# Reordering the loads and the rounding of weights in the fill of an eight-stage software pipeline

## The reference, cut to what matters

```python
    x = x + _L0_attn_a_ref(_layernorm(x, axis=-1), ...)   # q, k, v, gate; scan over t; Wo; W1, gelu, W2
    x = x + _L0_ffn_ref(_layernorm(x, axis=-1), L0_ffn_router_w, L0_ffn_expert_weights)
    x = x + _L0_attn_b_ref(_layernorm(x, axis=-1), ...)   # h = tanh(x_t B + h A^T); y = h C W_out^T + b
    x = x + _L0_ffn_ref(_layernorm(x, axis=-1), L0_ffn_router_w, L0_ffn_expert_weights)

    # inside _L0_attn_a_ref
    h = _ln(x, ln_w, ln_b)
    ...
    x = x + o.reshape(Bb, Tt, HEADS * DV) @ Wo
    h2 = _ln(x, ln_w, ln_b)
    return x + jax.nn.gelu(h2 @ W1 + b1, approximate=False) @ W2 + b2
```

## Time and profile before

| | |
|---|---|
| median of three runs | 1781.47 us |
| the profiled execution | 1783.68 us, of it 1781.9 us from first to last instruction (the span) |
| PE busy | 1658.3 us, 93% of the span |
| DVE, ACT, POOL busy | 73%, 57%, 48% |
| mean granted TensorE clock | 0.966 of full |
| the chain that ended last, by engine | PE 76%, ACT 7%, DVE 5%, issue 5%, POOL 4%, DMA 1%, SP's queue 1% |
| DMA | 11.8% of 16 engines for SP's queue; 32 GB/s mean |

### The profile page before, as it was taken

How to read it: one execution, slowest core, us unless ns; L and a number is a source line. 1 busy time by engine, 2 the same in 40 slices (tenths; PEclk the granted TensorE clock), 3 DMA queues, 4 the chain that set the end, 5 groups by cost and what they waited for, 6 DMA issues and landing times.

```text
span 1781.9 us, 47524 instructions
## 1 busy us (share of the span) xinstructions
PE 1658.3 (93%) x15176; PEld 1406.3 (79%) x15176; DVE 1303.9 (73%) x4558; ACT 1009.2 (57%) x3694; POOL 858.7 (48%) x1293
## 2 busy tenths in 40 slices
PE   5488899999999999999999999999999999998876
PEld 3377788888888888888888888888888888887755
DVE  4456677787777777877778777787777777776554
ACT  4355566666565665655656656556566666554431
POOL 1355355554554555545545655455455554443211
PEclk8689899999999999999999999999999999999878
DMA  4211111011111110011111110111111101110000
GB/s 121 66 31 31 31 32 27 26 25 35 35 35 35 33 26 25 22 35 35 35 35 35 25 27 23 31 35 35 35 35 28 25 23 30 31 31 7 6 7 12
DMA packets 108174, 56.26 MB, mean 32 GB/s; under 512 B 73904, under 2 KB 107344, under 8 KB 107984
## 3 DMA queue, kind: packets, MB, share of 16 engines
q1 hardware_dynamic: 106464, 53.75, 11.8%
q10 hardware_dynamic: 1648, 1.72, 0.3%
HBM read 30.28 MB, written 16.78 MB: 26 GB/s over the span
## 4 chain that ended last, share of the span: by engine, by line
PE 76%; ACT 7%; DVE 5%; issue 5%; POOL 4%; DMA 1%; SPq 1%; ACTq 0%; POOLq 0%; DVEq 0%
PE ps L1130 57%; PE ps L1136 5%; PE ps L1173 4%; PE ps L1147 3%; PE ps L1198 2%; PE ps L1163 2%; PE ps L1161 2%; POOL r L386 1%; ACT ym L545 1%; PE ps L1417 1%; DVE hs L772 1%; DVE st L782 1%; PE ps L1193 1%; ACT ps L551 1%; ACT part L557 1%
## 5 line engine op out<-in xcount | busy, mean ns | idle before, releaser
L1130 PE MATMUL ps<-we,yT 128*128 128x512 f32 x3072 | 823.1, 412 | 0.0
L1130 PEld LDWEIGHTS ps<-we,yT 128*128 128x128 f32 x3072 | 548.4, 192 | 101.7
L539 ACT ACTIVATE h_lead<-ps 48x8 fp32r<-48x8 f32 x1024 | 174.4, 170 | 601.3 <-PE ps L1147 595.2
L772 DVE SCALAR_TENSOR_TENSOR hs<-ps,cst,h_lead 48x8 fp32r<-48x8 f32 x1024 | 222.7, 217 | 188.5 <-ACT ps L540 184.2
L1147 PEld LDWEIGHTS ps<-hs,aT 128*128 128x128 f32 x1024 | 196.2, 192 | 104.4 <-DVE hs L772 78.1
L1147 PE MATMUL ps<-hs,aT 128*128 128x8 f32 x1024 | 208.4, 204 | 38.5 <-DVE hs L772 37.9
L803 DVE SCALAR_TENSOR_TENSOR stage<-ps,coef,stage 128x256 f32<-128x256 f32 x384 | 184.1, 479 | 36.8 <-PE ps L1130 24.0
L414 POOL TENSOR_TENSOR part<-part 128x256 f32<-128x256 f32 x64 | 46.7, 730 | 332.7 <-ACT part L558 332.7
L803 DVE SCALAR_TENSOR_TENSOR acc<-ps,coef,acc 128x256 f32<-128x256 f32 x384 | 183.8, 479 | 12.4 <-POOL acc L416 5.3
L436 POOL TENSOR_TENSOR orstd<-omean,mhalf 128x32 f32<-128x32 f32 x32 | 174.1, 5440 | 2.7
L540 ACT ACTIVATE ps<-ps 48x8 f32<-48x8 f32 x1024 | 164.3, 160 | 0.0
(11 more groups left out here) (179 smaller groups left out, 3340.1 us busy)
## 6 DMA issues: line engine op xcount, KB each, us to landing
xin<-in_x SPq DMA_DIRECT2D x64, 128.0 KB
vrow<-vtok SPq DMA_DIRECT2D x32, 256.0 KB, 2.2
vx<-vrow SPq DMA_DIRECT2D x128, 64.0 KB, 2.0
sx<-smid SPq DMA_DIRECT2D x128, 64.0 KB
xag<-in_x SPq DMA_DIRECT2D x64, 128.0 KB
out<-stage SPq DMA_DIRECT2D x64, 128.0 KB
stage<-in_experts SPq DMA_DIRECT2D x1, 2048.0 KB, 8.9
stage<-in_Wvg SPq DMA_DIRECT2D x1, 512.0 KB, 5.3
```

What stands on the lines that cost most here:

```text
L539: a.activation(h_lead[:], ps[0:NB, BANK["RB"], k * B:(k + 1) * B], ACT.Tanh)
L772: v.scalar_tensor_tensor(hs[0:NB, :, k], h_whole, keeps_rest, h_lead[:].bitcast(F32), ALU.mult, ALU.subtract).then_inc(sem("rnn_h"), 1)
L1130: ins = t.matmul(dst, left(lp, c), right(rp, c), start=(n == 1), stop=(n == 3 * chunks))
```

## The change

Three things, all in the fill (iterations 0 to 4):

1. `load_x(xag, 0)` is issued right behind the early weights, ahead of the wait for them, and no longer in iteration 2.
2. SP's order. In iteration 1 xin of round 1 goes ahead of the last three late loads (`bin_`) and of the nine of A; in iteration 2 xin of round 2 goes ahead of the wait for `weights_rest` and of the load of the experts.
3. `split_experts` is cut in halves on ACT as well as on DVE: the first half in iteration 3, the second in iteration 4, at the same places of the two programs.

```diff
@@ -235,7 +235,7 @@
-        LEAD = {w: n + 1 for n, w in enumerate(("gate", "early", "recurrence_out", "late", "router", "experts"))}
+        LEAD = {w: n + 1 for n, w in enumerate(("gate", "early", "recurrence_out", "late", "router", "experts0", "experts"))}
@@ -310,12 +310,11 @@
             load_x(xin, 0, "x_loaded")
             for dst, src in early_sync:
                 sp.dma_start(dst, src).then_inc(sem("early"), 16)
+            load_x(xag, 0, "x_again")
             sp.wait_ge(sem("pads_zero"), 1)
             sp.wait_ge(sem("early"), EARLY)
-            for dst, src in late_sync:
+            for dst, src in late_sync[:6]:
                 sp.dma_start(dst, src).then_inc(sem("late"), 16)
-            for dst, src in recurrence_weights:
-                sp.dma_start(dst, src).then_inc(sem("a_loaded"), 16)
             sp.wait_ge(sem("spread_zero"), 1)
@@ -345,13 +344,18 @@
                     spread_state()
+                if live(it, 0) and not (isinstance(it, int) and it == 0):
+                    sp.wait_ge(sem("y0"), past(c0 - 1))
+                    load_x(xin, it, "x_loaded")
+                if isinstance(it, int) and it == 1:
+                    for dst, src in late_sync[6:]:
+                        sp.dma_start(dst, src).then_inc(sem("late"), 16)
+                    for dst, src in recurrence_weights:
+                        sp.dma_start(dst, src).then_inc(sem("a_loaded"), 16)
                 if isinstance(it, int) and it == 2:
                     sp.wait_ge(sem("weights_rest"), REST["late"])
                     sp.dma_start(stage[:].rearrange("p (c e d) -> p c e d", c=KC, e=E), wts["experts"]).then_inc(sem("experts"), 16)
-                if live(it, 0) and not (isinstance(it, int) and it == 0):
-                    sp.wait_ge(sem("y0"), past(c0 - 1))
-                    load_x(xin, it, "x_loaded")
-                if live(it, 2):
+                if live(it, 2) and not (isinstance(it, int) and it == 2):
                     sp.wait_ge(sem("res"), past(c2 - 1))
                     load_x(xag, it - 2, "x_again")
@@ -529,9 +533,10 @@
-            def split_experts():
+            def split_experts(c):
+                cols = slice(c * E * D, (c + 1) * E * D)
                 act.wait_ge(sem("experts"), 16)
-                a.activation(we[:, 0, :], stage[:], ACT.Copy).then_inc(sem("weights_lead"), 1)
+                a.activation(we[:, 0, cols], stage[:, cols], ACT.Copy).then_inc(sem("weights_lead"), 1)
@@ -682,8 +687,8 @@
-                    if isinstance(it, int) and it == 3:
-                        split_experts()
+                    if isinstance(it, int) and it in (3, 4):
+                        split_experts(it - 3)
@@ -773,7 +778,7 @@
-                dve.wait_ge(sem("weights_lead"), LEAD["experts"])
+                dve.wait_ge(sem("weights_lead"), LEAD["experts" if c else "experts0"])
@@ -969,9 +974,8 @@
-                    if isinstance(it, int) and it == 3:
-                        split_experts(0)
-                        split_experts(1)
+                    if isinstance(it, int) and it in (3, 4):
+                        split_experts(it - 3)
```

## The result

| | before | after |
|---|---|---|
| median of the runs | 1781.47 us | 1770.36 us (five runs, 1765.72 to 1771.34) |
| the profiled execution | 1783.68 us, span 1781.9 | 1765.72 us, span 1763.9 |
| PE busy | 1658.3 us, 93% | 1652.0 us, 94% |
| mean granted clock | 0.966 | 0.971 |

The ratio is 0.9932, interval 0.9917 to 0.9946: 11.1 us by the medians, 12.1 us by the ratio, 9.6 to 14.8 us by the interval. One of five runs of the kernel before (2021.09 us) and one of twelve of `e2_queue_order` (2017.77 us, at a mean granted clock of 0.74) fell in a slower state and are left out of every ratio; without them the two medians are 1781.25 and 1778.46 us. The forecast was 1768.0 us, 13.5 less.

A forecast was written before the change was run, and what follows sets the result against it. PE, 93% busy, bounds the whole span, but the chain through the first 120 us bounds the part changed. 10.2 + 0.6 + 3.7 - 1.0 = 13.5 us off the median 1781.5 gives 1768.0 us, range 1763.5 to 1773.

The forecast's parts named there:

- Part 1: Iteration 2, DVE's wait for xag of round 0: the early load lets `oss` begin 10.2 us earlier.
- Part 2: Iteration 1, xin of round 1 earlier and `bin_` later: 0.6 us gained, between +0.4 and +2.0.
- Part 3: Iteration 3, half the experts' rounding and subtraction: 3.7 us gained, limited by xag of round 1; bounds 2.2 and 3.9.
- Part 4: Iteration 4, where the experts' second halves come back: 1.0 us lost, bounds 0 and 2.2.
- 1.45 us are left over: Iteration 4: DVE's added 2.24 us subtraction ahead of `xmid`, less the 0.79 us of idle time before `yT`'s rest.
- The sum: Whole kernel: 10.2 + 0.6 + 3.7 - 1.0 = 13.5 us gained in the fill and carried to the end.
- near 102: Sign to look for in the changed profile: PE's first logits near 102 us.
- The early xag holds back the early weights: Rival, shared four DMA engines: late things move by up to 3.0 us, time 1770.2 us; chance 0.12.
- The clock of PE stays up: Rival, PE's work after the shortened idle gap runs at 2.4 GHz: time 1766.5 to 1765 us; chance 0.14.
- Given back in the fill: Rival, iterations 3 and 4: xag of round 1 or second halves cost their upper bounds, 1770.7 us; chance 0.09.
- Another wait takes the place: Rival, the stall of iteration 2: PE's attention or the experts end it, not xag; about 1780 us; chance 0.03.
- slower by the late weights: Rival, iteration 1: `bin_` landing after 35.2 us holds `scale_out` and loses the gain; 1786 us at 40; chance 0.02.

The follow-up runs named there:

- e2_queue_order: Kernel before with only SP's new order: xin of round 1 ahead of `bin_` and A, xin of round 2 ahead of the experts; 1778.91 us, ratio 0.9991.
- e1: Kernel before with only xag of round 0 issued early, behind the early weights; 1771.68 us, ratio 0.9954.
- e5: The changed kernel run once more, unedited, for the size of chance; 1770.56 us, ratio 0.9934.
- e4: Changed kernel without the halves of the experts' rounding, so early xag and SP's new order only; 1771.93 us, ratio 0.9953.
- e7: Changed kernel with both expert halves in iteration 3: ACT's behind the lead of `oTs`, DVE's behind `y1` and `ge`; 1768.4 us, ratio 0.992.
- e3: Kernel before with only the experts rounded in halves, in iterations 3 and 4; 1777.85 us, ratio 0.9984.
- e6: Changed kernel with `scale_out` moved from iteration 1 to iteration 2, behind `qt`; 1770.42 us, ratio 0.9928.
- e9: e7 with `scale_out` in iteration 2 and xag of round 1 issued ahead of xin of round 3; 1766.71 us, ratio 0.99.
- e10: e9 with DVE's two expert subtractions elsewhere in iteration 3, ahead of `att` and behind `y1`, away from POOL's `omean`; 1760.88 us, ratio 0.9892.

## Why the prediction was right, and where it was wrong

**Part 1, right.** The stall went whole, `oss` stood at 42.35 and waited for `osq`, as named. `e1` has 9.2 to 9.95 us in the traces where 10.2 were forecast. Its share in the time, 8.2 us, has 10.2 within its interval.

**Part 2, right.** The prediction had two ends: `scale_out` at 21.4 us, which leaves the 2.0, and `bin_` landing at 23.2, which leaves 0.45. It took 0.6, near the second. `scale_out` began at 22.47 in the first trace of the changed kernel, and at 23.23, 23.34 and 23.51 in the three others with parts 1 and 2 that leave it in its place (`e5`, `e4`, `e7`), each time behind a wait for `bin_`: the late landing is what happened. `kt` stood at 25.81, 26.58, 26.68 and 26.85 in these four, and at 26.71 to 27.11 in the four traces without either part, 0.3 us apart on average. The 1.3 us between the first two traces are the most favourable pair. At the first `orstd` the part is worth 0.94 us by `e4` against `e1`, and 1.5 and 1.7 by the two traces of the changed kernel, all in the range of +0.4 to +2.0.

**Part 3, right.** 3.7 us were forecast. The plain differences at the second `orstd`, 4.08 in `e3` and 4.59 in the changed kernel against `e4`, take in what the traces already differed by at the first. From the first `orstd` to the second it took 33.89 to 34.40 us in six traces with the experts rounded in one iteration, 34.19 in `e4`, and 30.37, 30.49 and 30.55 in the changed kernel, `e5` and `e3`. So the part is worth 3.3 to 4.0 us, and 3.8 against `e4`. (`e6`, with halves too but `scale_out` in iteration 2, took 31.64; why is open.) The wait for xag of round 1 that was named as late next is there, 2.62 us; it was forecast as some 2. `e9` took it away.

**Part 4, mis-sized.** The step was "1.45 us are left over", less 0.4 of PE's own attention: 1.0. PE waited 2.90 us for `yT`, against 0.71 and 0.76 without the halves, so the wait grew by some 2.2. Two things had been left out. The subtraction took 3.39 us and not 2.28, since POOL's `res` ran beside it:

```profile
95.27 1.27 POOL L496 TENSOR_TENSOR res<-xag,b 128x512 f32<-128x512 f32 x1
```

It was 3.39 in both traces of the changed kernel, and 3.35 in `e6`. In `e3`, where it lay beside `res` for 0.94 us (109.97 to 110.91), it took 3.08, 0.80 longer. No kernel moved `res` away from it, so this cause rests on how the lengths go together. And PE had nothing left to cover with: at a granted clock of 1.00 from 87 to 95 us, it ended its attention at 98.16, 2.90 ahead of the logits:

```profile
97.53 0.63 PE L1202 MATMUL ps<-vx,att 128*32 128x64 f32 x32
```

The full clock seems also to have paid it back, though no kernel tests this: from the second `orstd` to the first logits the changed kernel took 27.01 us (27.14 in `e5`), the kernel before 26.43 and 28.04 in its two traces, and `e4` 27.47, whose PE ran at 0.50 from 94 to 98 us:

```profile
94.00:98.00 4.00, 4.00 (x42) 3.86 (x42) 1.43 (x2) 0.00 (x0) 1.33 (x3) 0.50 0.44 84
```

So the wait was twice what was forecast, and no loss up to the logits stands clear of what two traces of one kernel differ by. That the sum held all the same is luck. A price for part 4 in time is not to be had from these runs: against the first trace of the kernel before it is 0.6 us in the changed kernel and 3.84 in `e3`, and which of them depends on where PE's clock was low.

**The sum.** At the first logits 14.60 us were won where 13.5 were forecast, and "near 102" was 101.06. The medians give 11.1, with 9.6 to 14.8 by the interval; 13.5 lies in it. The 2.4 us between forecast and median are no more than one run differs from the next.

**The rivals.** *The early xag holds back the early weights*: refuted in its size, up to 3.0 us, and not in its kind. ACT's early rounding began at 9.94 to 10.45 us in the five traces without the early xag, and at 10.64 to 11.40 in the eight with it. All eight are later than all five, by 0.8 us on average; the 0.19 us of the first pair is the smallest difference. It did not wait for all of xag: in the changed kernel it began at 10.64, while DMA still moved at the share of 0.27 to 0.28 that it had held from 8.5 us on (before, nothing moved from 10.0 to 10.5 us):

```profile
9.00:9.50 0.50, 0.00 (x0) 0.00 (x0) 0.16 (x2) 0.00 (x0) 0.14 (x1) 1.00 0.28 90
10.50:11.00 0.50, 0.00 (x0) 0.00 (x0) 0.00 (x0) 0.36 (x1) 0.32 (x2) 1.00 0.27 94
```

Of the prediction's two readings, a small delay and a wait of Wk for all of xag, the traces bear out the first, at 0.8 us. The sum had this cost at nothing; whatever it cost is contained in the 9.2 to 9.95 us of part 1. *The clock of PE stays up*: refuted where it was said. After a gap of 5.88 us (15.0 before) PE worked from 51.0 to 54.7 us at 0.50:

```profile
51.00:54.70 3.70, 3.47 (x11) 2.80 (x11) 0.93 (x3) 1.71 (x4) 3.22 (x9) 0.50 0.00 0
```

It stayed up elsewhere, around 90 us, for which no rival had been made, and in sum less time was spent at the lower level (the last section has the figures). *Given back in the fill*: part 4 alone was at its upper bound, and part 3 was not. *Another wait takes the place*, and *slower by the late weights*: no; `scale_out` was 1.1 to 2.1 us later than its 21.4 in the four traces, and 13.8 were needed.

## What to carry to other kernels

Moving a load forward wins the wait of its consumer up to the point where the next input is ready, here 10.2 of 11.1 us by the forecast and 9.2 to 9.95 by the traces: read that from the timelines of the other engines before asking what the move will bring. When work is moved into an engine's idle time, look at what the neighbour does in that stretch too, as DVE and POOL can stop each other, and a place that is idle on one may be the path of the other. And when one pair of traces is compared, believe a mark in the first iterations, where both agree to some tenths, more than the spans; and before a difference of half a us is read from one pair, set it against every other trace of the same stretch.

## What the runs showed that was not expected

**DVE and POOL stopped each other.** POOL's `omean` on 128x32 took 0.25 us alone and 2.45 beside a DVE subtraction of 2.29, in `e7` (74.77, beside one at 74.85) and in `e9`. DVE's subtraction took 3.39 us beside a `res` of 1.27, 1.11 longer. In either case one of the two ran at its usual length and the other gave way. POOL was first by the profile both times, by 0.08 and 0.03 us, and gave way once, so who does is not settled by these rows. The Trainium skill ("SBUF — State Buffer", who interferes with whom) says that a DVE instruction with two SBUF inputs contends with a GpSimd instruction that reads SBUF; both pairs here are of that kind, and the trace agrees. Moving the subtraction away (`e10`) took `omean` back to 0.25, which shows the cause for this pair; for the other no kernel tried it. The same pair with one DVE input in PSUM was not tried.

**The granted clock differs between executions of one program.** It never fell below full between the fill's end (400 us) and 1580 us in any trace, and the stretch from the eighth `orstd` to the last took 1216.7 us in both traces of the kernel before, 1216.0 and 1216.9 in those of the changed one. Before 400 us the sum of the time at the lower level was 71.7 and 85.3 us in two traces of the kernel before, and 58.0 in both of the changed one. So the 18.0 us between the two profiled spans are 14.6 of the fill, 0.8 of the loop and 2.6 of the drain, and the last of these is of the size of chance: the two traces of the changed kernel differ by 2.2 us there.
